# A count on GpSimd for every row scatter, and a wait for the count of the last but one

## The reference

```python
xn = _layernorm(x, axis=-1)
x = x + _L0_attn_ref(xn, ...) + _L0_ffn_ref(xn, w_gate, w1, w3, w2)

# _L0_ffn_ref
logits = xt @ w_gate
top_logits, sel = jax.lax.top_k(logits, TOP_K)
probs = jax.nn.softmax(top_logits, axis=-1).astype(x.dtype)
h = jax.nn.silu(jnp.einsum('td,edh->eth', xt, w1)) * jnp.einsum('td,edh->eth', xt, w3)
y = jnp.einsum('eth,ehd->etd', h, w2)
yk = y[sel.T, t_idx[None, :], :]
out = jnp.einsum('ktd,tk->td', yk, probs)
```

## Time and profile before

| | us |
|---|---|
| median of 3 runs | 474.22 |
| lowest and highest | 473.81, 474.67 |
| the profiled execution, whole | 472.82 |
| its span, first to last instruction | 471.0 |
| GpSimd busy in it | 311.1 (66%) |
| TensorE busy in it | 428.5 (91%) |
| granted TensorE clock, share of full speed | 0.99 |

### The profile page before, as it was taken

The page is one execution under the profiler, slowest core; times in us unless marked ns, Lnnn a source line. Parts: engine busy times, 40 slices in busy tenths (PEclk is TensorE's granted clock), DMA queues, the critical chain, the costliest instruction groups (busy, mean ns, idle before and its releaser), DMA issues.

```text
span 471.0 us, 8361 instructions
## 1 busy us (share of the span) xinstructions
PE 428.5 (91%) x2440; PEld 306.9 (65%) x2440; DVE 394.9 (84%) x836; ACT 289.3 (61%) x406; POOL 311.1 (66%) x344
## 2 busy tenths in 40 slices
PE   0889969999999999998999999999999999989771
PEld 0877524555545555554888889889888998644461
DVE  5999985999999999997998997767767775699981
ACT  2793476788898888899364444344444553878710
POOL 3657777777777777660377777777777777776300
PEclk9999999999999999999999999999999999999997
DMA  8951126122121313143667766566556662019996
GB/s 244 290 174 43 52 101 188 52 66 81 52 92 51 97 52 97 35 119 109 171 204 218 231 203 191 177 186 189 168 159 188 179 181 89 21 52 226 210 214 147
DMA packets 48078, 65.93 MB, mean 140 GB/s; under 512 B 8424, under 2 KB 30223, under 8 KB 48048
## 3 DMA queue, kind: packets, MB, share of 16 engines
q1 hardware_dynamic: 36240, 39.56, 30.1%
q0 software_dynamic: 10656, 24.47, 18.6%
q10 hardware_dynamic: 1152, 1.57, 1.1%
HBM read 42.09 MB, written 33.83 MB: 161 GB/s over the span
## 4 chain that ended last, share of the span: by engine, by line
PE 48%; DVE 33%; issue 11%; ACT 5%; DMA 1%; DVEq 0%; SPq 0%; ACTq 0%
PE PD L893 13%; DVE hbuf L1398 6%; PE PB L725 4%; DVE hbuf L1409 4%; PE PD L836 3%; PE PA L859 3%; PE PB L855 3%; PE PA L855 3%; PE PB L859 3%; PE PB L856 3%; PE PA L856 3%; DVE gbuf L1380 3%; DVE y L1418 2%; DVE gbuf L1283 2%; DVE xacc L1496 2%
## 5 line engine op out<-in xcount | busy, mean ns | idle before, releaser
L608 POOL DMA_INDIRECT moe_out<-xnT,dst_u x142 | 147.2, 1036 | 63.4 <-issue 33.7
L593 POOL DMA_INDIRECT moe_in<-xn,slot_u x128 | 132.3, 1034 | 44.6 <-issue 39.1
L1196 ACT ACTIVATE xn<-PA 128x1024 f32<-128x1024 f32 (+1 forms) x36 | 36.5, 1015 | 64.3 <-PE PA L859 54.9
L893 PE MATMUL PD<-xnT,xn 128*128 128x128 f32 x536 | 65.7, 275 | 0.0
L1623 DVE TENSOR_TENSOR xn<-xn,PB 128x1024 f32<-128x1024 f32 (+1 forms) x36 | 43.4, 1205 | 25.5 <-PE PB L859 20.5
L893 PEld LDWEIGHTS PD<-xnT,xn 128*128 128x128 f32 x536 | 62.8, 192 | 0.5 <-issue 0.5
L740 PE MATMUL PC<-xc,Wc 128*128 128x512 f32 x128 | 57.8, 594 | 2.9 <-ACT xc L1093 2.9
L753 PE MATMUL PA<-xnT,Wtap 128*128 (+4 forms) x128 | 58.2, 598 | 0.0
L753 PEld LDWEIGHTS PA<-xnT,Wtap 128*128 128x128 f32 x128 | 24.9, 194 | 31.6 <-issue 31.6
L740 PEld LDWEIGHTS PC<-xc,Wc 128*128 128x128 f32 x128 | 23.2, 190 | 26.8 <-issue 23.4
L1486 DVE SCALAR_TENSOR_TENSOR acc<-PA,cw,acc 128x510 f32<-128x510 f32 (+2 forms) x48 | 35.5, 740 | 1.8 <-ACT acc L1082 1.4
(11 more groups left out here) (244 smaller groups left out, 922.9 us busy)
## 6 DMA issues: line engine op xcount, KB each, us to landing
xnT<-moe_w SPq DMA_DIRECT2D x36, 256.0 KB
xn<-moe_in SPq DMA_DIRECT2D x31, 266.0 KB
out_dram<-moe_out POOLq DMA_DIRECT2D x12, 512.0 KB, 15.3
xnT<-moe_w SPq DMA_DIRECT2D x36, 128.0 KB, 2.1
out_dram<-xacc SPq DMA_DIRECT2D x7, 512.0 KB, 3.5
moe_out<-xnT,dst_u POOLq DMA_INDIRECT x142
moe_in<-zrow SPq DMA_DIRECT2D x8, 266.0 KB, 3.5
moe_w<-in_L_ffn_w_dram SPq DMA_DIRECT2D x2, 1024.0 KB
```

The lines of the kernel that those rows point to most:

```text
L593: gp.indirect_dma_start(xs_dram, bass.IndirectOffsetOnAxis(ap=slot_u[:, k, j:j + 1], axis=0), xn_row[:, j, :], None).then_inc(s_scat, 16)
L608: gp.indirect_dma_start(yt_dram, bass.IndirectOffsetOnAxis(ap=dst_u[:, t, j:j + 1], axis=0), yo[t % OUTS][:, j, :], None, bounds_check=lim ...
L893: last = pe.matmul(PD[:, 512 + j * D:512 + (j + 1) * D], hid[b][:, k * SLOTS + j * P:k * SLOTS + (j + 1) * P], (w2x[t - FULL] if mixed and ...
L1196: act.activation(halves(sil, t), halves(PA[:, :], t), ACT.Silu).then_inc(s_sil, 1)
```

## The change

Each scatter gets a second semaphore, `s_desc`, passed as `engine_sem`: GpSimd itself adds 1 when the scatter has completed on it. The count of the DMA engines (`s_scat`, `s_ys`) stays. From the third scatter on, each waits until `s_desc` shows that the last but one has completed (`BEHIND = 2`). The numbering runs through both places: a scatter at L608 waits for `TOP_K * TILES` plus its own number. Lines below L247 move down by 2 to 6.

```diff
+BEHIND = 2
...
+        s_desc = sem("s_desc")
...
                         follow(j * TOP_K + k)
+                        if j * TOP_K + k >= BEHIND:
+                            gp.wait_ge(s_desc, j * TOP_K + k + 1 - BEHIND)
                         gp.indirect_dma_start(xs_dram, bass.IndirectOffsetOnAxis(ap=slot_u[:, k, j:j + 1], axis=0),
-                                              xn_row[:, j, :], None).then_inc(s_scat, 16)
+                                              xn_row[:, j, :], None, engine_sem=s_desc).then_inc(s_scat, 16)
...
+                    gp.wait_ge(s_desc, TOP_K * TILES + t * GT + j + 1 - BEHIND)
                     gp.indirect_dma_start(yt_dram, bass.IndirectOffsetOnAxis(ap=dst_u[:, t, j:j + 1], axis=0),
-                                          yo[t % OUTS][:, j, :], None, bounds_check=limit, oob_is_err=False).then_inc(s_ys[t % OUTS], 16)
+                                          yo[t % OUTS][:, j, :], None, bounds_check=limit, oob_is_err=False,
+                                          engine_sem=s_desc).then_inc(s_ys[t % OUTS], 16)
```

## The result

The changed kernel takes 475.88 us (median of 20 runs, 474.24 to 476.88), the kernel before 473.96 us in the same comparison (20 runs, 472.83 to 475.89). The ratio is 1.0038, with a 95% interval of 1.0025 to 1.0052: slower by some 1.8 to 1.9 us, where no change was forecast and 0.2% was taken as the limit of what can be told.

A forecast was written before the change was run, and what follows sets the result against it. The prediction took GpSimd's back-to-back scatters, with the last L608 scatter setting the end, as the bound. Counts of 0 to 1.6 us, taken as 0, and covered waits left 472.8 us profiled, 474.2 us as median; range 472.8 to 478.2 us.

The forecast's parts named there:

- a small price on each scatter: Rival at GpSimd's back-to-back scatters: each pays over 0.007 us; 486 us at 0.05, 507 at 0.13; chance 0.16.
- The forecast of no change: Whole kernel: 474.2 us, the same time as before; chance 0.69, with the wait that does nothing included.
- What bounds the kernel, and the one-for-one end: GpSimd's serial scatters: the last L608 scatter moves the end one for one, later without limit, earlier by at most 3.4 us.
- The count at 0: Each scatter's count on GpSimd: 0 to 0.01 us, taken as 0.
- The wait, covered by one scatter: Scatter n's wait for n-2 is hidden behind n-1: 1.56 us against a way of 0.31 or 0.78 us; no cost.
- The late count: Rival: the count comes when rows have landed; pitch 1.52 and 1.41 us, +41 us, 515 us in all; chance 0.05.
- What queues behind: GpSimd's queue, cut from a dozen scatters to one: worth nothing, since what was queued could not start sooner than its turn.
- I am wrong if the pitch of the scatters moves by 0.01 us or more: Test of the forecast on the spacing of GpSimd's scatters, 1.26 and 1.29 us, since the end would move with it.
- What would show it: Signs: gaps of 0.30 us, durations 0.96 and 0.98, last scatters near 209.5 and 420, L612's wait within two scatters of the last.
- the wait does nothing: Rival: the count is made when the scatter is handed on, so no wait holds; again 474.2 us, within the forecast's 0.69.
- fewer long scatters: Rival: a deep queue causes the long scatters and the 3.14 us hole; shortening it gains 3.4 us, giving 470.8; chance 0.10.
- The limit for no change: About 0.2%, 0.95 us, taken as what a measurement of this kernel can tell from no change.

The follow-up runs named there:

- the first profile: Profiled execution of the changed kernel from the main comparison, 476.87 us, against 472.82 us for that of the kernel before.
- the last pair: Changed kernel, 474.38 us (ratio 1.0022), and the same without the waits of scatters 224 to 247, 473.93 us (0.9999); kernel before 474.00 us.
- the first tail: Changed kernel plus 896 scatters behind its end: no wait, then waits for the second, fourth, eighth before; 958 ns long, 0.305 us apart in all parts.
- `BEHIND = 1`: Changed kernel, each scatter waiting for the count of the one just before instead of the last but one; ratio 1.0860 to the kernel before.
- the idle waits: Kernel before plus the change's 213 separate wait instructions, on a semaphore reached long before, no count; ratio 1.0120, six runs.
- The second tail: Kernel before plus 1024 scatters behind its end: 532-byte rows, then 512-byte rows plain, counted, and counted with the wait; gaps of 3.1 us every 113.

## Why the prediction was wrong

The measured 475.88 us lies inside the range of 472.8 to 478.2, but by luck: that part of the range stood for a small price on each scatter, which isn't there. The forecast of no change was wrong.

**What bounds the kernel, and the one-for-one end: right.** A last scatter 4.0 us later moved the end by 4.1 in the first profile; 1.5 us moved it by 1.5 in the last pair.

**The count at 0: right.** Predicted 0 to 0.01 us for each scatter, measured 0 to 1 ns in the first tail.

**The wait, covered by one scatter: right for the usual scatter, in mechanism and in size.** It gave 0.78 us for the way from a released wait to the start of a scatter that has a separate wait instruction. `BEHIND = 1` took the cover away, and the usual gap, the count's delay and that way together, was 0.76 to 0.79 us: the way alone, so that the count comes with the scatter's end. With `BEHIND = 2` the usual gap stayed 0.30. The late count, which needed over 0.78 us of delay on top, is excluded by the same rows.

**What queues behind: this step failed.** It said that what was queued "could not start sooner than its turn", and that a queue cut from a dozen to one is "worth nothing by itself". This holds only if each scatter is ready to be handed on when its turn comes. Once in 113 it is not: in the trace after, the sequencer's wait instructions for numbers 241 and 242 are these,

```profile
L612 POOLq EVENT_SEMAPHORE  x2: 17/17/17, 381.6 to 384.3; - x2
```

Number 239, which the first one waits for, had ended at 381.57, so that wait was through at once, and number 240, which the second one waits for, ended at 382.86. No count held the sequencer, and yet it got to the second only 2.7 us after the first, where the usual distance is the pitch of 1.29; number 241 started 0.2 us later. Nor did number 241's own wait for TensorE (`s_h1`) hold it: the product that it waits for had ended at 371.2. In the prediction's terms, the way from a released wait to a start, taken as 0.78 us for every scatter, is 2.9 us for number 241. The 1.56 us that one scatter covers leave 1.3 us of it open. Before the change the queue covered all of it. It wasn't a dozen there, as at the end, but eight: number 240 was let go 10 us before it started, right after VectorE had ended its buffer (370.1), with seven scatters ahead of it that had not started. The term missing from the sum is therefore +1.3 us, once in the second phase. The first phase's gap at number 113 was 3.14 us before and 3.28 after: it was uncovered in both. Why handing on takes so long once in 113 is open.

**The sign to look for was in the rows.** The forecast named a hole of 3.14 us ahead of number 113 and used it in a rival for a gain: a deep queue might cause it. The right question was the other one: if handing on stalls once in the first stage, why not in the second, of equal length, and what hides it there? The answer there, the queue, is exactly what the change removes. The rows before the change could raise the question but not answer it.

**"I am wrong if the pitch of the scatters moves by 0.01 us or more"** was too narrow. The usual pitch did not move by a nanosecond (0.30 and 0.96, 0.98 us, medians 1264 and 1288 ns), and the forecast was still wrong. Of **What would show it**, the wait at L618 one scatter ahead of the last and the last L597 scatter (209.94, for "near 209.5") held; the last L613 scatter, at 423.0 in one profile and 421.6 in the other for "near 420", did not. The sign that it named for the late count, idle time that ends on a scatter, came too (39.8 us) and meant nothing: at 0.30 us that idle time is no longer than before.

**Of the rivals**, that the wait does nothing is excluded by the sequencer's position, fewer long scatters by the first profile, and a small price on each scatter got the sign and the place right (no spare time behind the second phase), but not the form: it is one price of 1.3 us, not 270 small ones. The limit for no change was 0.95 us, so this single gap alone passes it.

## What to carry to other kernels

In this kernel a queue that runs ahead had no value while every step took its usual time; its value was the one long delay that it hid. Before shortening one, look for the rare long gap in stretches where the queue is already short, ask whether it is periodic, and add what it costs where the queue is now deep. When the limit must be kept, leaving it out for the few instructions around such a place can give the time back, as it did for the gap here.

Two profiles of one pair can differ by twice what the kernels do; a difference that doesn't return in a second profile of the same kernel belongs to the execution.

## What the hardware showed that was not expected

- After every 113 scatters of 128 rows that follow one another, GpSimd's next one starts after a gap of 3.1 us instead of 0.30 on an idle core, with rows of 512 or 532 bytes, plain, counted or waited for. In the experts' stage the gap is 1.5 to 2.9 us with a short queue, and nothing where the scatter ahead had been let go 2.4 us or more before its turn. What the 113 count, and why a long queue hides it there but not in the tails, is open.
- On number 241 the way from its wait instruction to its start is 2.9 us in nine of the ten traces that have such an instruction for it (3.9 in that of the idle waits), with one scatter queued or none, against 0.7 for a usual one with none.
- The count by `engine_sem` is as good as free: 958 ns and 0.305 us, with any wait or none, in the first tail.
- A wait for the scatter just before costs 0.45 to 0.48 us a scatter, that for the last but one nothing in the usual case.
- On an idle core plain scatters of 512-byte rows settled at 1.10 us and 0.30 between, and with the wait for the last but one at 0.98 and 0.42: the same 1.40 us, told in the one case as work and in the other as idle time. The second tail, its parts two (plain) and four (with the wait):

```profile
984.21 1.09 POOL L639 DMA_INDIRECT junk<-zrow,slot_u  x1 [0.30 <-issue]
985.61 1.10 POOL L639 DMA_INDIRECT junk<-zrow,slot_u  x1 [0.30 <-issue]
989.80 0.98 POOL L639 DMA_INDIRECT junk<-zrow,slot_u  x1 [3.10 <-issue]
...
1599.41 0.98 POOL L639 DMA_INDIRECT junk<-zrow,slot_u  x1 [0.42 <-DMA junk<-zrow,slot_u]
1600.81 0.98 POOL L639 DMA_INDIRECT junk<-zrow,slot_u  x1 [0.42 <-DMA junk<-zrow,slot_u]
```
